# Attention scores with the matrix product in three fp16 parts, and half of the score sums on ScalarE

## The chip, the cores and the metric

The kernel runs on one core of a Trainium2 chip. The metric is the device time of one execution in microseconds (us), taken as the median of several runs. The core has a matrix engine (TensorE, in the profile PE), a vector engine (VectorE, DVE), an activation engine (ScalarE, ACT), a general engine that also issues the indirect DMAs (GpSimd, POOL) and an engine that issues plain DMAs and waits (SyncE, SP). The engines run their own instruction streams and meet at semaphores.

## The reference, cut to what matters

Four graph layers run over 3125 nodes with 64 features and 103125 edges sorted by destination. The change lies in the fourth layer, in its attention scores:

```python
h = jnp.maximum(_layernorm(x, axis=-1), 0.0)
gl = (h @ W_l).reshape(n, 6, 64)
gr = (h @ W_r).reshape(n, 6, 64)
s = jax.nn.leaky_relu(gl[src] + gr[dst], 0.2)
e = jnp.einsum('ehf,hf->eh', s, att)     # one score per edge and head
# softmax of e over the edges of each dst, then a weighted sum of gl[src]
```

## The kernel before, in words

The scores are made by `edge3a` (from line 1920). Edges are taken in tiles of 128 and batches of eight tiles (B = 8, 1024 edges); 101 batches are used. Two batches make a pair t, and n = 2t + h + 1 is the batch number. For each batch:

- POOL gathers the rows of the source nodes with eight indirect DMAs (`Gather.gather`, L892) into one of four buffers `src_rows`. Before a batch it waits in L890 for its indices, for `hcTp_ready` (the batch four before must have been turned, so that the buffer is free) and for the copy of that buffer to HBM.
- SP loads the destination numbers (L1957) and eight windows of node rows (L1960) for the batch after the next, once `hcTp_ready` says that the buffers are free. It also stores the gathered rows (`kept`, L1977) and loads gather indices (L878).
- PE `turn` (L2031, L2032): sixteen matmuls put the features of both ends of all edges of a batch, transposed, into PSUM (`both_ends_t_ps`, one buffer of 128 x 1024): destination rows picked out of the window by a one-hot matrix, source rows by the identity. Its last matmul increments `hcTp_ready`.
- ACT `turned` (L2079) copies that to SBUF (`both_ends_t`, fp32, two buffers) and increments `hcT_ready`.
- PE `project` (L2040): per tile one fp32 matmul of 128 x 128 by 128 x 396 (Wz: six heads of 66 columns), two tiles for each step q = 0 to 3, into two alternating PSUM buffers `z_ps`. It increments `z_ready`.
- DVE `weigh` (L2133): relu of z times `att_z`, one instruction of 128 x 792 for each q, into `terms`; increments `terms_ready`, which frees the `z_ps` buffer.
- DVE `sum_terms` (L2141): a reduce over the 66 columns for half a batch, twice in a batch, into `scores`; it increments `summed`.
- PE `turn_scores` (L2047) turns the scores of the batch before, ACT copies them out of PSUM (L2085) and issues their store (L2087).
- DVE also makes the one-hot matrix of the batch after the next (L2125) and copies eight window numbers (L2118).

The order on PE within the body of batch n is written out by hand: project 0, project 1, turn of batch n + 1, turn_scores of n - 1, project 2, project 3. PE increments its semaphores in that order. DVE's order is weigh 0, weigh 1, sum, one-hot, weigh 2, weigh 3, sum. ACT's is `turned` of n + 1, then the store of n - 1.

## Time and profile before

| | us |
|---|---|
| median of three runs | 6714.87 |
| lowest and highest run | 6709.61, 6737.81 |
| the profiled execution | 6677.32 |
| its span (first to last instruction) | 6675.1 |
| the score stage in it, from the first gather (4624.65) to the last DVE sum (5908.85) | 1284.2 |
| busy in the span: PE, DVE, POOL, ACT | 4704.2, 4170.2, 3155.2, 1888.7 |

A row of the timeline gives the start in us from the span's start, the duration, the engine, the source line, the operation, output and inputs, how many instructions are merged into it, and in brackets how long the engine was idle before it and what ended that. The releaser in brackets is inferred. A wait named "DMA edge_edge_attr<-in_ea" in this stage is put under the name of a transfer of another stage. An fp32 matmul stands in the trace as two records. Matmul starts are recorded, their ends are modelled. PEclk is the granted clock of TensorE in tenths of full speed: it has two levels, 1.2 and 2.4 GHz, and a number in between is the mean of a stretch.

### The profile page before, as it was taken

What the parts mean: (1) busy time and instruction counts of PE and PEld (TensorE: products, weight loads), DVE (VectorE), ACT (ScalarE), POOL (GpSimd) and SP (SyncE); (2) the same over time, 40 slices, a digit from 0 to 9 for tenths busy, and PEclk for the clock granted to TensorE, in tenths of its full rate; (3) what the DMA queues carried; (4) which work ended last, traced back from release to release, by engine and by line L of the source; (5) the groups of instructions that cost most, each with busy time, mean ns of one, the idle gap of its engine ahead of it and who ended that gap; (6) DMA issues with size and microseconds to landing.
All of it is one profiled execution on the core that took longest, in us unless ns stands there. A gap on an engine that the chain in (4) does not pass through costs nothing. (4 is left out here: it accounts for less than half of the span.)

```text
span 6675.1 us, 100965 instructions
## 1 busy us (share of the span) xinstructions
PE 4704.2 (70%) x28624; PEld 3007.3 (45%) x28624; DVE 4170.2 (62%) x7653; ACT 1888.7 (28%) x6318; POOL 3155.2 (47%) x2946
## 2 busy tenths in 40 slices
PE   3777777777777676667566666663777777739998
PEld 2333333333334333333344554452444444418997
DVE  4454444444446666666666666664666766688997
ACT  1333333333333000000133333331000000016775
POOL 3433343333331655555354454452666666515554
PEclk7778787888888788888677878886999888869999
DMA  3222222222221111111111111111443334411111
GB/s 84 55 54 51 53 56 52 52 51 54 55 54 32 38 38 38 39 39 36 26 41 38 41 40 38 41 40 32 108 111 108 110 110 117 110 49 51 49 49 34
DMA packets 492408, 379.08 MB, mean 57 GB/s; under 512 B 345930, under 2 KB 378971, under 8 KB 492339
## 3 DMA queue, kind: packets, MB, share of 16 engines
q1 hardware_dynamic: 394803, 288.65, 15.3%
q0 software_dynamic: 90560, 83.37, 7.0%
q10 hardware_dynamic: 6976, 6.23, 0.3%
q8 instruction: 33, 0.54, 0.0%
q14 instruction: 36, 0.29, 0.0%
HBM read 341.76 MB, written 36.12 MB: 57 GB/s over the span
## 5 line engine op out<-in xcount | busy, mean ns | idle before, releaser
L1009 POOL DMA_INDIRECT edge_src_rows<-table_wh,edge_gather_idx x806 | 787.1, 977 | 1169.5 <-DVE edge_small L1128 924.6
L1038 PE MATMUL edge_sums_ps<-edge_onehot_src,edge_halves 128*128 128x512 bf16 x4840 | 1048.3, 361 | 302.5 <-issue 296.5
L892 POOL DMA_INDIRECT edge3a_src_rows<-table_h,edge3a_gather_idx x808 | 764.3, 946 | 564.1 <-issue 311.2
L2040 PE MATMUL edge3a_z_ps<-Wz,edge3a_both_ends_t 128*128 128x396 f32 x1616 | 695.3, 579 | 365.2 <-DVE edge3a_terms L2133 315.1
L1114 DVE TENSOR_SCALAR edge_onehot_src<-layer_node_row,edge_src_col,edge_magnitude 128x1568 bf16<-128x1568 f16 x605 | 410.5, 679 | 842.8 <-remote 471.6
L892 POOL DMA_INDIRECT table_cat<-table_hn,table_gather_idx x592 | 599.5, 1013 | 631.6 <-PE edge_cat_t_ps L1720 340.4
L1401 POOL DMA_INDIRECT edge_src_rows<-table_h,edge_gather_idx x608 | 606.9, 998 | 553.9 <-PE edge_msg_ps L1433 190.8
L1038 PEld LDWEIGHTS edge_sums_ps<-edge_onehot_src,edge_halves 128*128 128x128 f16 x4840 | 428.0, 104 | 872.7 <-issue 537.7
L2133 DVE SCALAR_TENSOR_TENSOR edge3a_terms<-edge3a_z_ps,att_z 128x792 f32<-128x792 f32 x404 | 386.0, 977 | 406.1 <-DMA edge_edge_attr<-in_ea 223.9
L2040 PEld LDWEIGHTS edge3a_z_ps<-Wz,edge3a_both_ends_t 128*128 128x128 f32 x1616 | 333.5, 217 | 670.1 <-DVE edge3a_terms L2133 359.6
L2452 PE MATMUL edge3b_sums_ps<-edge3b_onehot,edge3b_weighted 128*128 128x128 f32 x4848 | 572.7, 278 | 6.2 <-DVE layers_accT L2490 4.5
L2452 PEld LDWEIGHTS edge3b_sums_ps<-edge3b_onehot,edge3b_weighted 128*128 128x128 f32 x4848 | 553.5, 193 | 11.8 <-DVE layers_accT L2490 4.7
L1416 PE MATMUL edge_src_rows_t_ps<-edge_onehot_src,edge_h_halves 128*128 128x512 f16 x1300 | 375.1, 431 | 230.4 <-DVE edge_onehot_src L1522 149.2
L2369 POOL TENSOR_TENSOR edge3b_weighted<-edge3b_src_rows,edge3b_alpha 128x1920 f32<-128x1920 f32 x101 | 350.3, 3468 | 344.9 <-DVE edge3b_alpha L2469 251.2
L2418 ACT ACTIVATE edge3b_weighted<-edge3b_src_rows,edge3b_alpha 128x64 f32<-128x64 f32 x1818 | 445.1, 334 | 166.1 <-DVE edge3b_alpha L2469 157.3
L1736 PE MATMUL edge_msg_ps<-rR,edge_cat_t 64*128 64x128 f32 x1616 | 180.7, 388 | 371.8 <-DVE edge_u L1861 255.4
L1066 ACT ACTIVATE edge_dst_rows<-edge_dst_rows_ps 128x390 f32<-128x390 f32 x153 | 70.4, 460 | 1293.1 <-DMA scores_by_head<-setup_zeros 928.5
L2079 ACT ACTIVATE edge3a_both_ends_t<-edge3a_both_ends_t_ps 128x1024 f32<-128x1024 f32 x101 | 103.5, 1024 | 1161.9 <-DMA edge_edge_attr<-in_ea 690.4
L1038 PE MATMUL edge_sums_ps<-edge_onehot_src_act,edge_halves 128*128 128x512 bf16 x1608 | 336.6, 340 | 77.0 <-issue 76.6
L2141 DVE TENSOR_REDUCE edge3a_scores<-edge3a_terms 128x24 f32<-128x1584 f32 x202 | 364.5, 1805 | 7.0
L1023 PE MATMUL edge_dst_rows_ps<-edge_window,edge_onehot_t 128*128 128x65 f32 x1632 | 263.0, 314 | 121.8 <-issue 82.8
L1875 DVE TENSOR_TENSOR layers_accT<-layers_accT,edge_sums_ps 65x128 f32 x808 | 198.7, 280 | 236.7 <-remote 217.7
(372 smaller groups left out, 8320.9 us busy)
## 6 DMA issues: line engine op xcount, KB each, us to landing
edge_dst_row<-in_dst_row SPq DMA_DIRECT2D x102, 512.0 KB
edge3a_dst_row<-in_dst_row SPq DMA_DIRECT2D x102, 512.0 KB
edge_window<-table_wh SPq DMA_DIRECT2D x816, 32.5 KB
edge3a_window<-table_h SPq DMA_DIRECT2D x816, 32.0 KB
edge_edge_attr<-in_ea SPq DMA_DIRECT2D x101, 256.0 KB
kept_rows<-edge3a_src_rows SPq DMA_DIRECT2D x101, 256.0 KB
edge3b_src_rows<-kept_rows SPq DMA_DIRECT2D x101, 256.0 KB
edge_edge_attr<-in_ea SPq DMA_DIRECT2D x101, 128.0 KB
```

What stands on the lines that cost most here:

```text
L892: nc.gpsimd.indirect_dma_start(self.slot(b, j), None, self.table[:, :], bass.IndirectOffsetOnAxis(ap=self.idx[b][:, j:j + 1], axis=0)).the ...
L1009: nc.gpsimd.indirect_dma_start(g[q][:, j, :], None, k.t_wh[:, :], bass.IndirectOffsetOnAxis(ap=idx[q][:, j:j + 1], axis=0)).then_inc(gathe ...
L1038: mm = pe.matmul(acc[:, i, 0:w], halves[q][:, j, a, :, :].rearrange("p h d -> p (h d)"), hot[:, o:o + w], start=first and a == 0, stop=False)
L1114: dve.tensor_scalar(slot_v(q, j)[:, :], k.node_row[:, :], col[q][:, j:j + 1], mag[q][:, j:j + 1], ALU.is_equal, ALU.mult).then_inc(hot_v, 1)
L1401: nc.gpsimd.indirect_dma_start(g[p][:, j, :], None, k.t_h[:, :], bass.IndirectOffsetOnAxis(ap=idx[p][:, j:j + 1], axis=0)).then_inc(gather ...
L1416: mm = pe.matmul(rowsTp[:, o:o + 512], h16[:, b, :], ring[b % RING][:, o:o + 512], start=(b == 0), stop=(b == NB - 1))
L2040: mm = pe.matmul(zp[q % 2][:, i, 0:H * ZH], hcT[h][:, j * P:(j + 1) * P], k.Wz[:, :], start=True, stop=True)
L2133: dve.scalar_tensor_tensor(terms[:, 2 * q:2 * q + 2, :], zp[q % 2][:, :, 0:H * ZH], 0.0, rows_over(k.att_z[:, :], 2), ALU.max, ALU.mult).t ...
L2141: dve.tensor_reduce(scs[h][:, :, j:j + B // 2].rearrange("p h b -> p b h"), terms[:, j:j + B // 2, :].rearrange("p b (h f) -> p b h f", h= ...
L2369: return engine.tensor_tensor(hp[h][:, a:b, :, :], rows, weights, ALU.mult)
L2418: w = act.activation(hp[h][:, j, a, :], st[h][:, j, :], ACT.Copy, scale=al[h][:, a, j:j + 1])
L2452: mm = pe.matmul(sums[j % 4][:, i, :], hp[h][:, j, 2 * i:2 * i + 2, :].rearrange("p a d -> p (a d)"), oh[h][:, j, :], start=True, stop=True)
```

## The change

The product with Wz is made from 16-bit parts. Both Wz and the turned rows are scaled by powers of two (LIFT is 4096; Wz also by a power of two found from its largest magnitude) and split into a high fp16 part and a low fp16 part, the rest. Three fp16 matmuls per tile, high by high, high by low and low by high, accumulate in PSUM in place of one fp32 matmul. ACT makes the high part of the rows (as before, but into fp16 and scaled). DVE makes the low part with a new instruction `lower` of 128 x 1024, which reads PSUM and the high part; PE's projections wait for it. The scales are taken back in `att_z`. A chain of small steps over ACT, DVE and PE before the first batch finds the power of two and splits Wz; PE's first `turn` stands behind it. The sums over the 66 columns are divided: DVE reduces tiles 0 to 3, and ACT sums tiles 4 to 7 with 24 ACTIVATEs of 128 x 66 that write their sum through `accum_out`. `turn_scores` and the later `weigh` wait for both.

```diff
-                        mm = pe.matmul(zp[q % 2][:, i, 0:H * ZH], hcT[h][:, j * P:(j + 1) * P],
-                                       k.Wz[:, :], start=True, stop=True)
+                        out, cols = zp[q % 2][:, i, 0:H * ZH], slice(j * P, (j + 1) * P)
+                        pe.matmul(out, hiT[h][:, cols], Whi[:, :], start=True, stop=False)
+                        pe.matmul(out, hiT[h][:, cols], Wlo[:, :], start=False, stop=False)
+                        mm = pe.matmul(out, loT[h][:, cols], Whi[:, :], start=False, stop=True)
...
                 def turn_scores(n, h):
                     pe.wait_ge(scT_ready, n)
-                    pe.wait_ge(summed, 2 * n + 4)
+                    pe.wait_ge(summed, n + 2)
+                    pe.wait_ge(summed_act, n + 2)
...
+                pe.wait_ge(most_ready, 1)
+                pe.matmul(scTp[0:1, 0:P], most[:, 0:1], k.ident[:, :], start=True, stop=True).then_inc(most_turned, 1)
+                pe.wait_ge(power_ready, 1)
+                pe.matmul(zp[0][:, 0, 0:1], ones[:, :], most[0:1, 2:3], start=True, stop=True).then_inc(power_spread, 1)
+                pe.wait_ge(W_ready, 2)
                 turn(1, 0, 1, 0, 0)
...
-                    act.activation(hcT[h][:, :], hcTp[:, :], ACT.Copy).then_inc(hcT_ready, 1)
+                    act.activation(hiT[h][:, :], hcTp[:, :], ACT.Copy, scale=LIFT).then_inc(hi_ready, 1)
+
+                def sum_terms(n, h):
+                    act.wait_ge(scTp_ready, n)
+                    for q in (2, 3):
+                        act.wait_ge(terms_ready, 4 * (n - 1) + q + 3)
+                        for j in (2 * q, 2 * q + 1):
+                            for f in range(H):
+                                last = act.activation(terms[:, j, f * ZH:(f + 1) * ZH], terms[:, j, f * ZH:(f + 1) * ZH], ACT.Copy,
+                                                      accum_out=scs[h][:, f, j:j + 1])
+                    last.then_inc(summed_act, 1)
...
+                        sum_terms(n, h)
...
-                    dve.wait_ge(summed, 2 * n + q // 2 + 1)
+                    dve.wait_ge(summed if q < 2 else summed_act, n + 1)
...
+                def lower(n, h):
+                    dve.wait_ge(hi_ready, n)
+                    dve.scalar_tensor_tensor(loT[h][:, :], hcTp[:, :], LIFT, hiT[h][:, :], ALU.mult,
+                                             ALU.subtract).then_inc(hcT_ready, 1)
...
                         weigh(n, 2)
+                        if not empty(last, h + 1):
+                            lower(n + 1, 1 - h)
                         weigh(n, 3)
-                        sum_terms(n, h, 1)
```

## Rows read from the trace of the kernel before

**Rows 1.** The page: busy time of each engine, and the clock in 40 slices.

```profile
PE 4704.2 (70%) x28624; PEld 3007.3 (45%) x28624; DVE 4170.2 (62%) x7653; ACT 1888.7 (28%) x6318; POOL 3155.2 (47%) x2946
PEclk7778787888888788888677878886999888869999
```

**Rows 2.** Groups by line, 4700 to 5900 us: busy, mean ns | idle before, releasers.

```profile
L892 POOL DMA_INDIRECT edge3a_src_rows<-table_h,edge3a_gather_idx x756 | 715.1, 946 | 454.6 <-issue 288.4 <-DMA edge_edge_attr<-in_ea 141.3 <-DMA kept_rows<-edge3a_src_rows 15.2
L2040 PE MATMUL edge3a_z_ps<-Wz,edge3a_both_ends_t 128*128 128x396 f32 x1563 | 672.5, 579 | 326.9 <-DVE edge3a_terms L2133 307.8 <-issue 18.8
L2133 DVE SCALAR_TENSOR_TENSOR edge3a_terms<-edge3a_z_ps,att_z 128x792 f32<-128x792 f32 x391 | 373.7, 977 | 359.6 <-DMA edge_edge_attr<-in_ea 217.9 <-PE edge3a_z_ps L2040 89.2 <-issue 52.1
L2141 DVE TENSOR_REDUCE edge3a_scores<-edge3a_terms 128x24 f32<-128x1584 f32 x196 | 353.7, 1805 | 6.7
L2125 DVE TENSOR_TENSOR edge3a_onehot_t<-edge3a_dst_row,edge3a_window_nodes_ps 128x1024 f32<-128x1024 int32 x98 | 118.6, 1211 | 0.0
```

**Rows 3.** Timeline of POOL: last and first gathers of two batches.

```profile
5306.15 0.95 POOL L892 DMA_INDIRECT edge3a_src_rows<-table_h,edge3a_gather_idx  x1 [0.30 <-issue]
5309.69 0.95 POOL L892 DMA_INDIRECT edge3a_src_rows<-table_h,edge3a_gather_idx  x1 [2.59 <-DMA edge_edge_attr<-in_ea]
5318.45 0.95 POOL L892 DMA_INDIRECT edge3a_src_rows<-table_h,edge3a_gather_idx  x1 [0.30 <-issue]
5321.65 0.95 POOL L892 DMA_INDIRECT edge3a_src_rows<-table_h,edge3a_gather_idx  x1 [2.26 <-issue]
```

**Rows 4.** Timeline of PE, same batch: last matmul of the turn, then projections 2 and 3.

```profile
5304.83 0.27 PE L2032 MATMUL edge3a_both_ends_t_ps<-ident,edge3a_src_rows 128*64 128x128 f32 x1
5305.25 3.23 PE L2040 MATMUL edge3a_z_ps<-Wz,edge3a_both_ends_t 128*128 128x396 f32 x8
```

**Rows 5.** Timeline of DVE and ACT, same batch.

```profile
5303.24 0.98 DVE L2133 SCALAR_TENSOR_TENSOR edge3a_terms<-edge3a_z_ps,att_z 128x792 f32<-128x792 f32 x1 [1.14 <-issue]
5308.98 1.02 ACT L2079 ACTIVATE edge3a_both_ends_t<-edge3a_both_ends_t_ps 128x1024 f32<-128x1024 f32 x1 [11.08 <-PE edge3a_z_ps L2040]
5309.08 1.87 DVE L2133 SCALAR_TENSOR_TENSOR edge3a_terms<-edge3a_z_ps,att_z 128x792 f32<-128x792 f32 x2 [1.90 <-PE edge3a_z_ps L2040]
5310.31 0.73 ACTq L2087 DMA_DIRECT2D scores_by_head<-edge3a_scores_t  x1
```

**Rows 6.** Timeline at the stage's start: PE, POOL, ACT.

```profile
4639.21 0.42 PE L2032 MATMUL edge3a_both_ends_t_ps<-ident,edge3a_src_rows 128*64 128x128 f32 x1
4663.42 0.95 POOL L892 DMA_INDIRECT edge3a_src_rows<-table_h,edge3a_gather_idx  x1 [0.30 <-issue]
4669.61 1.02 ACT L2079 ACTIVATE edge3a_both_ends_t<-edge3a_both_ends_t_ps 128x1024 f32<-128x1024 f32 x1 [54.05 <-DMA edge_edge_attr<-in_ea]
```

**Rows 7.** Timeline at the stage's end: POOL's last gather, then PE and ACT.

```profile
5868.33 0.94 POOL L892 DMA_INDIRECT edge3a_src_rows<-table_h,edge3a_gather_idx  x1 [0.30 <-issue]
5878.55 0.27 PE L2032 MATMUL edge3a_both_ends_t_ps<-ident,edge3a_src_rows 128*64 128x128 f32 x1
5878.95 1.02 ACT L2079 ACTIVATE edge3a_both_ends_t<-edge3a_both_ends_t_ps 128x1024 f32<-128x1024 f32 x1 [6.63 <-PE edge3a_both_ends_t_ps L2032]
5886.88 1.03 ACT L2079 ACTIVATE edge3a_both_ends_t<-edge3a_both_ends_t_ps 128x1024 f32<-128x1024 f32 x1 [6.75 <-PE edge3a_both_ends_t_ps L2032]
```

**Rows 8.** Timeline of ACT elsewhere: sums through `accum_out`, and small ACTIVATEs within SBUF.

```profile
3435.89 0.22 ACT L1756 ACTIVATE edge_squares<-edge_msg_ps 128x64 f32<-128x64 f32 x1
3435.99 0.20 ACT L1756 ACTIVATION_READ_ACCUMULATOR edge_squares<-edge_msg_ps 128x1 f32 x1
3436.08 0.23 ACT L1756 ACTIVATE edge_squares<-edge_msg_ps 128x64 f32<-128x64 f32 x1
6105.15 4.41 ACT L2418 ACTIVATE edge3b_weighted<-edge3b_src_rows,edge3b_alpha 128x64 f32<-128x64 f32 x18 [1.41 <-DVE edge3b_alpha L2469]
```

**Rows 9.** Nearest relatives of the new work: fp16 matmuls, and a DVE instruction on PSUM.

```profile
2200.44 0.60 PE L1416 MATMUL edge_src_rows_t_ps<-edge_onehot_src,edge_h_halves 128*128 128x512 f16 x2 [0.72 <-DVE edge_onehot_src L1522]
L1526 DVE TENSOR_TENSOR edge_onehot<-dst_rel,edge_columns_ps 128x1024 f32<-128x1024 f32 x101 | 123.3, 1221 | 350.8 <-remote 320.8 <-PE edge_sums_ps L1443 28.4
```

More of the change, by code:

```diff
@@ L1928, in edge3a @@
         oht = [c.sb(f"onehot_t{h}", [P, ROWS]) for h in (0, 1)]
-        hcT = [c.sb(f"both_ends_t{h}", [P, ROWS]) for h in (0, 1)]
+        hiT = [c.sb(f"both_ends_high{h}", [P, ROWS], F16) for h in (0, 1)]
+        loT = [c.sb(f"both_ends_low{h}", [P, ROWS], F16) for h in (0, 1)]
+        Wz = c.sb("Wz_scaled", [P, H * ZH])
+        Whi = c.sb("Wz_high", [P, H * ZH], F16)
+        Wlo = c.sb("Wz_low", [P, H * ZH], F16)
+        ones = c.sb("ones", [1, P])
+        most = c.sb("largest", [P, 4])
+        prep, abs_ready, most_ready, most_turned, power_ready, power_spread, scaled_ready, W_ready = c.sems(
+            "prep_step", "magnitudes_ready", "largest_ready", "largest_in_psum", "power_ready", "power_in_psum",
+            "scaled_ready", "Wz_parts_ready")
+        hi_ready, summed_act = c.sems("high_ready", "terms_summed_by_scalar")
         terms = c.sb("terms", [P, B, H * ZH])
@@ L2088, in store @@
                                   scT[h][:, :]).then_inc(stored[h], 16)
+                act.activation(Wz[:, :], k.Wz[:, :], ACT.Abs).then_inc(abs_ready, 1)
+                act.wait_ge(scaled_ready, 1)
+                act.activation(Whi[:, :], Wz[:, :], ACT.Copy).then_inc(W_ready, 1)
                 turned(1, 0)
@@ L2135, in weigh, with sum_terms @@
                                              ).then_inc(terms_ready, 1)
-                def sum_terms(n, h, half):
-                    dve.wait_ge(terms_ready, 4 * (n - 1) + 2 * half + 4)
+                def sum_terms(n, h):
+                    dve.wait_ge(terms_ready, 4 * (n - 1) + 4)
                     dve.wait_ge(scTp_ready, n)
-                    j = half * B // 2
-                    dve.tensor_reduce(scs[h][:, :, j:j + B // 2].rearrange("p h b -> p b h"),
-                                      terms[:, j:j + B // 2, :].rearrange("p b (h f) -> p b h f", h=H),
+                    dve.tensor_reduce(scs[h][:, :, 0:B // 2].rearrange("p h b -> p b h"),
+                                      terms[:, 0:B // 2, :].rearrange("p b (h f) -> p b h f", h=H),
@@ L2143, in sum_terms @@
                                       AX, ALU.add).then_inc(summed, 1)
+                def lower(n, h):
+                    dve.wait_ge(hi_ready, n)
+                    dve.scalar_tensor_tensor(loT[h][:, :], hcTp[:, :], LIFT, hiT[h][:, :], ALU.mult,
+                                             ALU.subtract).then_inc(hcT_ready, 1)
+                step = Chain(dve, prep)
+                step(dve.memset(ones[:, :], 1.0))
+                dve.wait_ge(abs_ready, 1)
+                dve.tensor_reduce(most[:, 0:1], Wz[:, :], AX, ALU.max).then_inc(most_ready, 1)
@@ new lines, in _ @@
+                dve.wait_ge(most_turned, 1)
+                step(dve.tensor_reduce(most[0:1, 1:2], scTp[0:1, 0:P], AX, ALU.max))
+                dve.tensor_scalar(most[0:1, 2:3].bitcast(I32), most[0:1, 1:2].bitcast(I32), EXPONENT, LEAST,
+                                  ALU.bitwise_and, ALU.bitwise_or).then_inc(power_ready, 1)
+                dve.wait_ge(power_spread, 1)
+                step(dve.tensor_copy(most[:, 0:1], zp[0][:, 0, 0:1]))
+                step(dve.tensor_scalar(most[:, 3:4].bitcast(I32), most[:, 0:1].bitcast(I32), EXPONENT, None,
+                                       ALU.bitwise_xor))
@@ L2145, in _ @@
+                dve.tensor_scalar(Wz[:, :], k.Wz[:, :], most[:, 3:4], LIFT, ALU.mult, ALU.mult).then_inc(scaled_ready, 1)
+                step(dve.tensor_scalar(k.att_z[:, :], k.att_z[:, :], most[:, 0:1], 0.5 / (LIFT * LIFT),
+                                       ALU.mult, ALU.mult))
+                dve.wait_ge(scaled_ready, 1)
+                dve.wait_ge(W_ready, 1)
+                dve.tensor_tensor(Wlo[:, :], Wz[:, :], Whi[:, :], ALU.subtract).then_inc(W_ready, 1)
                 nodes(1, 0, 0)
@@ L2148, in _ @@
                 onehot_t(2, 1, 0)
+                lower(1, 0)
                 def body(t, last):
```

7 lines of the change are left out of this document (4 added, 3 removed).

## The prediction

> **What bounds the kernel now.** The page comes first [rows 1]: no engine is busy throughout, and TensorE's clock is granted at eight tenths of full speed or more in most slices, so nothing can be read off the shares. The change lies in one stage, so the groups by line of its steady part come next [rows 2]. In 1200 us DVE makes 98 one-hots, one for each batch: a batch takes 12.2 us. The same rows give each engine's work per batch. POOL: 8 gathers. DVE: 4 x 0.977 + 2 x 1.805 + 1.21 and 0.16 for a small copy = 8.9 us. PE: the eight records of four fp32 projections start 0.33 us apart, 0.66 us for each tile [rows 4], so 5.3 us of projections, plus a turn. ACT: little. None of DVE, PE or ACT fills 12.2 us.
>
> The timeline of POOL tells what does [rows 3]. Seven steps lead from the first gather of a batch at 5309.69 to its last at 5318.45: 1.25 us each, 9.7 us from the first start to the last end at 5319.40. Then POOL waits 2.26 us and starts again at 5321.65. The batch before is alike: last end 5307.10, next start 5309.69, 2.59 us. So a period of 12.0 us is 9.7 of gathers and 2.3 of waiting, and POOL waits for the turn of an earlier batch.
>
> Why is that turn late? By PE's own rows it isn't: its last matmul starts at 5304.83 and lasts 0.27, yet ACT, which waits for just this, wakes at 5308.98 [rows 4, 5]. DVE's weigh 2, which needs a projection recorded well before, wakes 0.1 us behind ACT, and weigh 3 follows with no gap [rows 5]. So the increments that PE owes from the turn onward (turn, scores, projections 2 and 3) all arrive in one burst, 1.9 us after POOL's last gather of the batch ended. The projections ahead of the turn arrive without such a delay: weigh 1 starts at 5303.24, amid gathers [rows 5]. The stage's two ends show that the gathers hold the burst back. At the start the first turn's last matmul is over at 4639.63, every engine but POOL is idle, and ACT wakes at 4669.61, after the last of 32 gathers, which ended at 4664.37 [rows 6]: 30 us of hold. At the end, with the last gather over at 5869.27, the turn's last matmul ends at 5878.82 and ACT starts at 5878.95: no hold, and the batches then come 7.93 us apart [rows 7]. I can't name the mechanism; the pattern is that a turn's increment becomes visible only when the outstanding gathers are done. That makes a lockstep: release, 0.7 us, eight gathers, 1.5 to 1.9 us, release. No engine's speed enters it as long as the turn is ready when the gathers finish.
>
> **The change part by part**, from a release R (5308.98 is one) to the next at R + 12.0.
>
> ACT makes the high part: 1.02 us, as now. Its score copy and DMA issue are over at 5311.04, R + 2.1 [rows 5]. DVE does weigh 2 to R + 1.1, then `lower`. The trace has none; its nearest row is a DVE instruction of 128 x 1024 that reads PSUM, 1.22 us [rows 9]. It ends at R + 2.4, where PE could start before at R + 1.1: 1.3 us later. Against that one reduce of 1.8 us goes, so DVE has 8.9 - 1.8 + 1.2 = 8.3 us of work. Bounds of `lower`: 0.98 us, one weigh of 792 columns, and 1.8 us, one reduce.
>
> PE: 24 fp16 matmuls for a batch in place of 8 fp32 ones. Two fp16 matmuls of 512 columns take 0.60 us, the last of them to its modelled end of 0.38, so 0.22 us apart [rows 9]; by columns 396/512 x 0.22 = 0.17 us. A tile costs 0.51 instead of 0.66, a batch 4.1 instead of 5.3. Upper bound: weight loads that don't overlap and a pitch of 0.32 as between the fp32 records, 7.7 us. The chain is then: project 0 from R + 2.4 to 3.4, project 1 (after weigh 3, R + 3.4) to 4.5, the turn, 1.7 us, to R + 6.2. It has to be done by R + 12.0: 5.8 us of slack. If the lighter load keeps the clock at its low level of 1.2 GHz, projections take 2.0 each and the turn 3.4: R + 9.9, still inside.
>
> ACT's 24 sums: in the two-instruction form that `accum_out` makes, starts of pairs are 0.19 to 0.20 us apart (3435.89 to 3436.08) though each lasts 0.22 and 0.20: they overlap [rows 8]. So 24 x 0.20 = 4.8 us, from R + 2.1 to R + 7.0 (the terms come at R + 1.1 and 3.4). Those rows read PSUM; the new ones read and write SBUF. The nearest row for that, 18 ACTIVATEs in 4.41 us, gives (4.41 - 0.33)/17 = 0.24 us apart [rows 8]; with the read's step of 0.1 on top 0.34, and 24 x 0.34 = 8.2, to R + 10.3. I take 0.20 to 0.34: both end before R + 12.0. Behind these sums are queued, on ACT, the next batch's high part, and on PE turn_scores and with it projections 2 and 3. At 0.20 scores follow at R + 7.1 and projection 3 is over by R + 9.5. At 0.34 it is over at about R + 12.6, where DVE wants it at R + 14.5 (after weigh 2 and `lower`). Nobody waits. The cover of all this is the hold; without it the chain would be DVE's 8.3 us or POOL's 10.0.
>
> The Trainium skill ("VectorE: DVE Perf Modes", section on the TRN2 errata of SBUF-source ops) speaks against moving many small sums to ScalarE: it gives 224 cycles fixed for SBUF to SBUF and 172 for PSUM to SBUF. By an estimate from that page a pair would be 52/1.2 = 43 ns dearer than the PSUM rows, 24 of them 1.0 us, and ACT would end at R + 8.0 and not 7.0; the sum would stay.
>
> Steady part: 98 batches x 0 us. Head: the steps that split Wz, a dozen small ones, some 6 us from 4621, lie ahead of a turn that starts near 4636 and is released at 4669.6 [rows 6]: 0. Should PE's two increments of this chain be held by the gathers as the turn's are, the first turn would come after 4669.6: + 8. That has a reason against it, projections aren't held. Tail: once POOL has stopped, three batches run at 7.93 us [rows 7], bound by DVE. There DVE saves 0.6 us a batch, `lower` stands between the release and the projections (up to 1.2 each), and the last 12 sums take 2.4 where the reduce took 1.8: between -2 and + 3, taken as 0. Sum: 0 us, with bounds of -2 and + 11.
>
> The profiled execution took 6677.3 us, 37.6 under the median of the runs; its new span would be 6675. On the median that is 6714.9, and I say 6715. About 0.5% (34 us) is what a measurement of this kernel can tell from no change; the runs themselves lie 28 us apart.
>
> **Rivals.** *ACT becomes the bound (slower).* From a pair of (12.0 - 2.1)/24 = 0.41 us upward ACT fills the period. If the accumulator read waits for its ACTIVATE and the next waits for it, a pair costs 0.24 + 0.23 = 0.47 us from the single durations: 2.1 + 11.3 = 13.4 us a batch, + 1.4 x 98 = 137 us, 6850. Against it: the overlapping starts [rows 8]. For it: reading and writing the same SBUF tile has no row.
>
> *The hold is not the gathers' but the pace of the chain (faster).* If PE's recorded starts mislead and its real work fills the time up to the burst, 1.2 us less of projections per batch shorten it: 6715 - 1.2 x 98 = 6597. If the hold vanished, POOL's 10.0 us would be the floor, 2.0 x 98 = 196 us less, 6519. Against it: 30 us of hold at the start with PE idle, and none at the end [rows 6, 7].
>
> *The projections don't get cheaper (no change).* At 0.32 us per fp16 matmul PE works 7.7 us instead of 5.3 and the turn is over near R + 8: the same 6715. Only the profile would show it.
>
> **How the numbers follow.** Forecast, with the third rival in it: 0.77. ACT-bound or a similar new wait: 0.12. Chain-bound or hold gone: 0.11. Range 6678 to 6752: the forecast's own, from the sum at the profiled execution's level (6677) to the highest run (6738) with the + 11 of the bounds; it leaves the two other cases out, which are too far to reach. Faster by over 0.5% 0.11, within 0.77, slower 0.12.
>
> **What would show it.** Right: gathers still 8 x 1.25 us with a gap of 2.3 to 2.6; ACT's high part still starts 1.5 to 1.9 us after the last gather; PE's turn recorded 4 us or more before; 24 pairs 0.20 to 0.34 us apart; PE's busy time in the stage down by a fifth; DVE's by 0.6 us a batch. Wrong: gathers waiting over 3 us while ACT is busy up to the next high part, or a gap of 0.3 us between batches on POOL, which would mean that the hold depended on the work that was changed.

## The result, and the profile after

The changed kernel takes 6836.97 us (median of 4 runs, 6821.48 to 6846.83) beside 6712.24 of before: a ratio of 1.0173, 95% interval 1.0147 to 1.0200, 125 us slower. Forecast were 6715 us and a range to 6752. The profiled executions took 6821.48 and 6677.32 us, 144 apart. From its first gather (4622.4) to its last instruction (6053.3) the score stage takes 1430.9 us; before it took 1285.0 by the same marks. No other stage changed by more than 23 us, in either direction.

The page, busy times and clock, to be held against [rows 1]:

```profile
PE 4677.8 (69%) x29284; PEld 2963.8 (43%) x29436; DVE 4109.1 (60%) x7662; ACT 2542.5 (37%) x11168; POOL 3147.6 (46%) x2946
PEclk6888888888787878887688788777877777868999
```

The groups by line, 4700 to 5900 us, to be held against [rows 2]:

```profile
L892 POOL DMA_INDIRECT edge3a_src_rows<-table_h,edge3a_gather_idx x694 | 656.4, 946 | 544.6 <-issue 270.5 <-DMA kept_rows<-edge3a_src_rows 211.3 <-PE edge3a_both_ends_t_ps L2042 62.9
L2105 ACT ACTIVATE edge3a_terms<-edge3a_terms 128x66 f32<-128x66 f32 x2077 | 505.6, 245 | 372.9 <-issue 320.7 <-DVE edge3a_terms L2166 50.1
L2166 DVE SCALAR_TENSOR_TENSOR edge3a_terms<-edge3a_z_ps,att_z 128x792 f32<-128x792 f32 x346 | 338.2, 979 | 508.3 <-remote 358.2 <-issue 124.8 <-PE edge3a_z_ps L2053 24.9
L2051 PE MATMUL edge3a_z_ps<-edge3a_Wz_high,edge3a_both_ends_high 128*128 128x396 f16 x690 | 294.5, 427 | 54.4 <-issue 43.1 <-DVE edge3a_both_ends_low L2179 11.4
L2158 DVE TENSOR_TENSOR edge3a_onehot_t<-edge3a_dst_row,edge3a_window_nodes_ps 128x1024 f32<-128x1024 int32 x87 | 105.3, 1210 | 0.0
```

87 one-hots in 1200 us instead of 98: 13.8 us a batch. PE and DVE are busy for a smaller share of the time, ACT for a larger one. POOL's gathers still last 946 ns, but its idle time rose from 454.6 to 544.6 us for fewer gathers, and a releaser that counted 15.2 us before now counts 211.3: the store of the gathered rows. ACT has a new idle time of 320.7 us, "issue", ahead of its sums and between them.

What that is shows in the timeline of ACT, sums of one batch (start, duration, [idle before]):

```profile
5305.03 0.24 ACT L2105 ACTIVATE edge3a_terms<-edge3a_terms 128x66 f32<-128x66 f32 x1
5305.27 0.24 ACT L2105 ACTIVATE edge3a_terms<-edge3a_terms 128x66 f32<-128x66 f32 x1
...
5307.58 0.26 ACT L2105 ACTIVATE edge3a_terms<-edge3a_terms 128x66 f32<-128x66 f32 x1 [0.50 <-issue]
5307.75 0.19 ACT L2105 ACTIVATION_READ_ACCUMULATOR edge3a_terms<-edge3a_terms 128x1 f32 x1
5308.32 0.26 ACT L2105 ACTIVATE edge3a_terms<-edge3a_terms 128x66 f32<-128x66 f32 x1 [0.39 <-issue]
5309.04 0.20 ACT L2105 ACTIVATION_READ_ACCUMULATOR edge3a_terms<-edge3a_terms 128x1 f32 x1 [0.46 <-issue]
5309.77 0.26 ACT L2105 ACTIVATE edge3a_terms<-edge3a_terms 128x66 f32<-128x66 f32 x1 [0.52 <-issue]
...
5313.14 1.00 ACT L2097 ACTIVATE edge3a_both_ends_high<-edge3a_both_ends_t_ps 128x1024 f16<-128x1024 f32 x1
...
5317.15 0.26 ACT L2105 ACTIVATE edge3a_terms<-edge3a_terms 128x66 f32<-128x66 f32 x1 [2.76 <-issue]
```

Pairs start 0.24 us apart, and then, from 5305.3 on, single instructions come 0.7 us apart (8.32, 9.04, 9.77), though each lasts a quarter of that and waits for no semaphore. I call these late steps. They end 1.5 us after POOL's last gather:

```profile
5299.10 0.94 POOL L892 DMA_INDIRECT edge3a_src_rows<-table_h,edge3a_gather_idx  x1 [5.20 <-DMA kept_rows<-edge3a_src_rows]
...
5309.43 0.95 POOL L892 DMA_INDIRECT edge3a_src_rows<-table_h,edge3a_gather_idx  x1 [0.30 <-issue]
5313.03 0.94 POOL L892 DMA_INDIRECT edge3a_src_rows<-table_h,edge3a_gather_idx  x1 [2.66 <-issue]
```

So what the prediction had seen as PE's increments held back is one face of something that slows ACT too, and SP: in the trace of before, from 4740 to 5560 us, 248 of the steps between SP's own instructions are 0.64 to 0.78 us long, and on a chip without late steps (e11 below, a stretch of 800 us) 15. In the batch above the turn's last matmul was recorded at 5307.25 and its count came at 5312.24. That is how it went throughout before (the count 4.85 us after the last record, median of 66 batches, the turn's records 1.70 us from first to last), but in the changed kernel it is the exception, 8% of the batches. In most, as in the next one, PE itself can be seen to stall inside the turn, whose records then stretch over 4.0 us (median of 59) with the count right behind them (timeline of PE):

```profile
5321.87 0.38 PE L2041 MATMUL edge3a_both_ends_t_ps<-edge3a_onehot_t,edge3a_window 128*64 128x128 f32 x2
5323.70 0.27 PE L2042 MATMUL edge3a_both_ends_t_ps<-ident,edge3a_src_rows 128*64 128x128 f32 x1 [1.45 <-issue]
5324.42 0.31 PE L2042 MATMUL edge3a_both_ends_t_ps<-ident,edge3a_src_rows 128*64 128x128 f32 x1 [0.45 <-issue]
```

**Where the 1.5 us of a batch lie.** Its eight gathers take 9.7 us in every kernel (once in some twelve batches a gap of 1.9 us falls behind the first of them, the same in all kernels), so a batch grows by POOL's pause between the batches alone. I cut each pause between 4740 and 5560 us in two, at the time when the turn's count (`hcTp_ready`) rises: from the end of the last gather to the count, and from the count to POOL's next start. Means in us, 60 to 66 pauses each, worked out from the semaphores' times in the traces; kernels named e are the experiments below; "late in sums" is by how much the steps from the first sum's start to the last one's exceed 0.24 us a pair. (With 24 sums the step from the twelfth to the thirteenth is in it, where ACT can also wait for weigh 3; without that step the changed kernel has 3.1.)

| kernel | pause | to the count | count to POOL | late in sums |
|---|---|---|---|---|
| before | 2.51 | 1.63 | 0.88 | |
| e1, three fp16 products, sums on DVE | 2.95 | 1.85 | 1.10 | |
| e2, fp32 products, sums on ACT | 3.44 | 2.11 | 1.33 | 3.3 |
| changed | 3.99 | 2.42 | 1.57 | 4.2 |
| e3, changed, scores turned last | 3.82 | 2.04 | 1.79 | 4.9 |
| e5, before without window loads | 2.68 | 1.86 | 0.82 | |
| e6, changed without window loads | 3.17 | 2.35 | 0.82 | 3.4 |
| e15, changed, 12 sums on ACT | 3.54 | 1.99 | 1.56 | 0.3 |
| e17, changed, kept rows stored earlier | 3.74 | 2.56 | 1.19 | 4.0 |

Of the 1.48 us by which the pause grew, 0.79 lie ahead of the count and 0.69 behind it.

### The profile page after: what moved, and what is told of

It reads as the page before. It is cut to its first block and busy times, and to the rows that moved or that the text cites. A ratio compares the mean times of both kernels' runs of the same rounds, so it can differ in the third digit from the quotient of the medians.

```text
span 6819.3 us, 107297 instructions
## 1 busy us (share of the span) xinstructions
PE 4677.8 (69%) x29284; PEld 2963.8 (43%) x29436; DVE 4109.1 (60%) x7662; ACT 2542.5 (37%) x11168; POOL 3147.6 (46%) x2946
## 5 line engine op out<-in xcount | busy, mean ns | idle before, releaser
L1038 PE MATMUL edge_sums_ps<-edge_onehot_src,edge_halves 128*128 128x512 bf16 (+1 forms) x4736 | 983.1, 354 | 213.8 <-issue 201.3
L2105 ACT ACTIVATE edge3a_terms<-edge3a_terms 128x66 f32<-128x66 f32 x2424 | 589.7, 245 | 421.1 <-issue 344.8
L2105 ACT ACTIVATION_READ_ACCUMULATOR edge3a_terms<-edge3a_terms 128x1 f32 x2424 | 457.6, 189 | 171.6 <-issue 171.0
L1416 PE MATMUL edge_src_rows_t_ps<-edge_onehot_src,edge_h_halves 128*128 128x512 f16 x1300 | 360.0, 418 | 183.3 <-DVE edge_onehot_src L1522 119.3
L1038 PE MATMUL edge_sums_ps<-edge_onehot_src_act,edge_halves 128*128 128x512 bf16 (+1 forms) x1560 | 338.6, 336 | 206.0 <-issue 201.3
L2051 PE MATMUL edge3a_z_ps<-edge3a_Wz_high,edge3a_both_ends_high 128*128 128x396 f16 x808 | 342.6, 424 | 101.6 <-DVE edge3a_both_ends_low L2179 52.0
L1486 ACT ACTIVATE edge_msg<-edge_msg_ps 128x512 f32<-128x512 f32 x101 | 60.3, 597 | 864.9 <-remote 597.6
L1077 ACT ACTIVATE edge_onehot_src_act<-edge_distance,edge_magnitude,edge_minus_magnitude 128x1568 bf16<-128x1568 f16 x201 | 340.4, 1694 | 15.6 <-PE edge_sums_ps L1038 5.3
```

Of the source, the lines that this page charges most:

```text
L1038: mm = pe.matmul(acc[:, i, 0:w], halves[q][:, j, a, :, :].rearrange("p h d -> p (h d)"), hot[:, o:o + w], start=first and a == 0, stop=False)
L1416: mm = pe.matmul(rowsTp[:, o:o + 512], h16[:, b, :], ring[b % RING][:, o:o + 512], start=(b == 0), stop=(b == NB - 1))
L2051: pe.matmul(out, hiT[h][:, cols], Whi[:, :], start=True, stop=False)
L2105: last = act.activation(terms[:, j, f * ZH:(f + 1) * ZH], terms[:, j, f * ZH:(f + 1) * ZH], ACT.Copy, accum_out=scs[h][:, f, j:j + 1])
```

## The experiments

They ran on several chips; each time is held against the kernel before on its own chip. Stages and batches, though, are read from one profiled execution of each kernel, and for the kernel before there is one such trace, from another chip.

### Which half of the change costs: e1, e2

e1 is the changed kernel with

```
-                        sum_terms(n, h)
...
+                        sum_terms(n, h, 1)
```

(the first line is ACT's, the second stands behind weigh 3 on DVE, for tiles 4 to 7) and e2 the kernel before with only the opposite edit.

> The changed kernel, but VectorE makes both halves of the sums again; the three fp16 products, the high and low parts and their scales stay. Theory A (the change's time comes from ScalarE's 24 sums, which lie in the chain sums, turning of the scores, projection 2, weigh 2, sums): about 6712 us as before, batches of edge3a 12.1 to 12.3 us. Theory B (the three-part product, its extra low-part step on VectorE and the lower granted clock are what costs): about 6835 us. If both carry something it lies between, near 6712 plus B's share.

> The kernel before (fp32 products), with one edit alone: ScalarE sums the terms of tiles 4 to 7. Theory A: the whole loss comes, 6835 us or somewhat more, with the same gaps between ScalarE's sums. Theory B: 6712 us or less, since VectorE is relieved of 1.8 us a batch and nothing else changes.

Measured beside 6659.65: e1 6729.12, ratio 1.0089 (1.0059 to 1.0119); e2 6763.25, ratio 1.0154 (1.0123 to 1.0186). The stage takes 1336.0 and 1381.3 us. Against 1285.0 of before that is 51 and 96 us; together 147, where the whole change costs 146. By the medians it is 69 and 104 us, together 173, where the whole change costs 125 (128 in e13). So both halves cost, and neither theory stands alone: some three fifths come with the sums, two fifths with the products. That the two add up exactly isn't shown.

### Is it the chain over the scores: e3

```
-                        if not (first and h == 0):
-                            turn_scores(n - 1, 1 - h)
                         project(n, h, 2)
                         project(n, h, 3)
+                        if not (first and h == 0):
+                            turn_scores(n - 1, 1 - h)
```

> The changed kernel, with PE's turning of the last batch's scores put behind projection 3 instead of ahead of projection 2, so that projections 2 and 3 no longer wait for ScalarE's 24 sums of the batch before. Theory A1 (it is that chain): the chain is broken at PE; weigh 2 still waits for the buffer that ScalarE read, but ahead of that the projection is done; 12.3 to 13.0 us a batch, 6715 to 6780 us. Theory A2 (ScalarE as such is full: its own work and its gaps make 13.7 us a batch in whatever order): 6835 us, unchanged.

6792.54 us, ratio 1.0204 (1.0171 to 1.0237), stage 1406.8, batch 13.6: A1's range is missed, and A2's "unchanged" came, though e15 will show that ACT isn't full. In the changed kernel PE waited for ACT's sums ahead of that step (5.85 us before turn_scores at 5313.38). With the wait moved, the table shows the count as early as in e15, and POOL even later behind it. The wait passed from PE to DVE: weigh 2 needs the tiles that ACT still sums, and by the waits of e3 (4700 to 5500 us) the weigh steps wait 178.6 us for ACT, in 52 batches, a wait that isn't among those of the changed kernel.

### Gathers: e4, and the same kernel without a pause between gathers, e12 and e14

e4: the changed kernel, `Gather` issues 4 gathers a batch instead of 8, all waits on them count 4. e12 and e14 are one kernel: before, but the gathers fill tiles that nobody reads, and POOL waits only for its own gathers of four batches ago:

```
-        wait_past(pool, self.free, 2 * t + h - 1)
-        if kept:
-            wait_past(pool, kept[b], 16 * m)
+        wait_past(pool, ga.gathered[b], B * 16 * m)
...
-                self.slot(b, j), None, self.table[:, :],
+                gd[b][:, j, :], None, k.t_h3[:, :],
```

> The changed kernel with 4 gathers a batch in edge3a instead of 8 (the rows of tiles 4 to 7 stay zero). Theory H (the stretch in which PE's count isn't let go and in which ScalarE's sums come 0.4 to 0.7 us apart ends 1.7 to 1.9 us behind the last gather, whatever makes it): that stretch ends 5 us sooner, the sums come 0.24 us apart almost throughout, and the batch falls by at least the 3 to 5 us that the gaps take, to 9 to 10.5 us: 6835 - 98 x 3.5 = about 6490 us. Rival (gaps and gathers only fall together by chance): the gaps stay, the batch stays near 13.7 us and the time near 6835 us.

e4: 6371.25 us beside 6659.65, 288 us less than before though it has all the sums. A batch takes 9.4 us; from the turn's first record to its count 2.0 us pass (median), where it is 6.8 before and 4.7 in the changed kernel; the sums lose 0.8 us a batch. Groups by line, 4700 to 5500 us:

```profile
L2111 ACT ACTIVATE edge3a_terms<-edge3a_terms 128x66 f32<-128x66 f32 x2045 | 494.4, 243 | 164.2 <-issue 136.4 <-DVE edge3a_terms L2172 27.5
L893 POOL DMA_INDIRECT edge3a_src_rows<-table_h,edge3a_gather_idx x341 | 322.5, 946 | 477.6 <-DMA kept_rows<-edge3a_src_rows 383.4 <-issue 85.1 <-PE edge3a_both_ends_t_ps L2048 9.0
```

> The kernel before, but edge3a's gathers fill tiles that nobody reads, and POOL waits for nothing but its own earlier gathers, so that it gathers without a pause from the stage's start (the turn reads constant tiles, the scores are of wrong rows). Theory K taken literally (PE's counts are held as long as any gather is under way): PE's counts come out only in the rare pauses, and the stage takes longer than its 1282 us, if it doesn't take twice as long. Rival M (a count is held only until the gathers that were queued at the time are done, or the hold needs the handshake between PE and POOL): the batches run at VectorE's pace of 8.5 to 9 us while POOL gathers at 10 us a batch, and the stage takes some 1010 us by POOL: about 6390 us.

> The kernel with unpaced gathers again (tiles that nobody reads, POOL waits for its own earlier gathers alone, the turn reads constant tiles), for a chip on which the kernel before takes some 6700 us. Theory K (PE's counts are late as long as any gather is under way): the stage takes longer than 1282 us. Rival M (the lateness needs the handshake between PE and POOL): the stage takes some 1010 us. On a chip without late counts it says nothing new: 1009 us as before.

e12 met a chip without late steps (below) and says nothing on them: 8.4 us a batch, VectorE's pace. e14 met one that has them: 7345.97 us beside 6736.61. The view by windows, first while POOL gathers without a pause, then after its last gather (busy us of PE, PEld, DVE, ACT, POOL; granted clock, DMA share, GB/s):

```profile
4650.00:5650.00 1000.00, 126.25 (x380) 58.50 (x380) 60.10 (x57) 9.80 (x14) 753.17 (x731) 0.52 0.16 34
5900.00:6500.00 600.00, 561.98 (x3554) 341.39 (x3552) 595.13 (x571) 83.58 (x142) 0.00 (x0) 1.00 0.42 130
```

and PE's timeline in the first:

```profile
5012.50 0.82 PE L2058 MATMUL edge3a_z_ps<-Wz,edge3a_both_ends_t 128*128 128x396 f32 x1 [2.01 <-issue]
5015.30 0.82 PE L2058 MATMUL edge3a_z_ps<-Wz,edge3a_both_ends_t 128*128 128x396 f32 x1 [1.98 <-issue]
5018.10 0.82 PE L2058 MATMUL edge3a_z_ps<-Wz,edge3a_both_ends_t 128*128 128x396 f32 x1 [1.98 <-issue]
```

Matmuls come 2.80 us apart, four steps of 0.7 (an fp32 projection has two loads and two matmuls), a batch takes 140 us, and once the gathers are over 8.4 us. PE waits for no semaphore between these matmuls, POOL doesn't look at its count, and the source rows that it turns are constant tiles. So gathers in a long row are enough to make PE's late steps; e4 shows that four in a row, with a pause behind them, make hardly any.

### Do the other transfers make them: e5 to e8

e5 and e6 are before and changed with the window tiles loaded for the first two batches only; e7 and e8 load 8 columns of dst_row instead of 1024 from the third batch on:

```
-                    for j, base in enumerate(window_starts(nc, k, SP, t, h)):
+                    for j, base in enumerate(window_starts(nc, k, SP, t, h)) if begin else ():
```

> The kernel before, but edge3a loads the 8 window tiles only for its first two batches and turns those again and again (so SP issues 3 transfers a batch instead of 11 and reads no window starts; the scores are of wrong rows). Theory W (the spells in which SP's and ScalarE's own steps come 0.7 us apart, and PE's count is late, come from the window loads beside the gathers): the spells go, PE's count goes out with the turn, and the batch falls from 12.1 us to what the gathers alone take, 8 x 1.25 plus at most 1 us: some 10.5 us, 6660 - 98 x 1.6 = about 6500 us. Theory G (the gathers alone make them): 12.1 us a batch and about 6660 us, unchanged.

> The same edit to the changed kernel. Theory W: ScalarE's 24 sums come 0.24 us apart throughout; batch 10.5 to 12 us, 6500 to 6650 us. Theory G: 13.7 us a batch, about 6810 us.

> The kernel before, but from the third batch on the load of dst_row brings 8 columns instead of 1024 (32 KB read and written instead of 512 KB; the one-hots of edge3a stay those of the first batches). Theory D (the spells come from the bytes that move beside the gathers): the spells shrink or go, 10.5 to 11.5 us a batch, 6500 to 6600 us. Theories W and G: unchanged, 12.1 us and about 6660 us.

> The same edit to the changed kernel. Theory D: batch below 12.5 us, below 6700 us. Theories W and G: 13.7 us a batch, about 6810 us.

Beside 6757.7: e5 6704.28, e6 6764.63, e7 6722.23, e8 6862.96, one run each, that of before too. Theories W and D fall: from the turn's first record to its count 3.9 us or more pass in all four (median), the batch of e5 is 12.5 us and not 10.5, and ACT's sums still lose 3.4 us in e6, beside 4.3 in e8. But e6 is faster than e8 by 98 us and has 13.0 us a batch, and the table says where: the count is as late as in the changed kernel, yet POOL starts 0.82 us behind it and not 1.57. Without window loads the change costs 60 us (e6 less e5), and all of it lies ahead of the count; with them it costs 141 (e8 less e7). POOL's waits, 4700 to 5500 us, show what is missing (us in total, times, longest): changed kernel, then e6:

```profile
POOL edge3a_src_rows L892 <- DMA kept_rows<-edge3a_src_rows: 135.4, 28, 5.6
POOL edge3a_src_rows L892 <- PE edge3a_both_ends_t_ps L2042: 45.6, 14, 3.5
```

```profile
POOL edge3a_src_rows L892 <- PE edge3a_both_ends_t_ps L2042: 96.6, 30, 3.9
```

The same view gives 4.6 us for that store before the change, 87.8 in e1 and 112.3 in e2. SP's queue explains it: the store stands behind eight window loads, which SP issues only when the count has come, and if these fall into late steps, the store goes out late. The timeline of SP in the changed kernel shows one such round:

```profile
5312.40 0.33 SPq L1967 DMA_DIRECT2D edge3a_dst_row<-in_dst_row  x1
5313.56 5.09 SPq L1970 DMA_DIRECT2D edge3a_window<-table_h  x8
5321.54 0.72 SPq L878 DMA_DIRECT2D edge3a_gather_idx<-in_src_t  x1
5324.38 0.00 SPq L1987 DMA_DIRECT2D kept_rows<-edge3a_src_rows  x1
```

and POOL, whose last gather had ended at 5322.73, starts again at 5325.79, released by that store.

### Sums and store, one at a time: e15, e17

e15 leaves 12 of the 24 sums on ACT, e17 issues the store one batch earlier in SP's queue:

```
-                    for q in (2, 3):
+                    for q in (3,):
...
-                                     g[b][:, :, :]).then_inc(kept[b], 16)
+                            keep(*behind_one(t, q, m, h))
```

> The changed kernel with half as much on ScalarE: it sums tiles 6 and 7 (12 pairs), VectorE sums tiles 0 to 5 (the second piece, tiles 4 and 5, behind weigh 3). Theory A' (the batch goes round by ScalarE: hi part 1.0, wait for low part and weigh 2 some 3, then the 24 sums, 5.8 by themselves and 2.7 of late steps): 12 pairs fewer take 2.9 us and half of the late steps out of the ring, 13.8 - 4.2 = 9.6, so that the gathers' handshake bounds again with what the fp16 products add: 12.4 to 12.7 us a batch as with all sums on VectorE, ratio 1.007 to 1.012. Theory B' (the loss of the sums' half is made by the extra hand-over between engines and not by the number of sums): 13.4 us a batch or more, ratio 1.015 or more.

> The changed kernel, with the store of the gathered rows (kept_rows) issued one batch earlier in SP's queue. In the changed kernel POOL waits 135 us of the 800 us from 4700 on for that store, 2 us a batch, against 5 us in all in the kernel before; it stands in SP's queue behind 8 window loads whose steps come 0.7 us apart while gathers run. Theory N (most of the loss comes by that store: everything behind PE is a little later, SP's loads fall into the late steps, the store lands late and POOL starts the next gathers late): a batch takes about 12.6 to 12.9 us instead of 13.8, ratio 1.005 to 1.010. Theory A' (ScalarE's ring of 24 sums bounds, POOL's wait is only another face of it): unchanged, 13.7 us, ratio 1.017 to 1.019.

e15: 6760.64 beside 6659.93, ratio 1.0155 (1.0129 to 1.0181). The changed kernel has 1.0173, and 1.0189 in e13; these intervals overlap, so the times alone don't show a gain. The batch takes 13.4 us. The sums now lie ahead of the late steps and lose 0.3 us a batch, ACT's high part starts 0.1 us behind the count and no longer 1.7 us, and the count is 0.43 us earlier, but POOL's start behind it is as late as in the changed kernel. That is the forecast of B' (13.4 us or more, ratio 1.015 or more): ACT's ring of sums doesn't carry the loss by itself. The view of POOL's waits puts 144.8 us of 800 to the store again; by which way the handed-over sums make it late here wasn't traced. e17: 6834.76 beside 6717.78, ratio 1.0148 (1.0096 to 1.0200), an interval that takes in the changed kernel. POOL's wait for the store is gone and another entry of SP's queue has taken its place (same view, 4700 to 5500 us):

```profile
POOL edge3a_src_rows L892 <- DMA edge3a_gather_idx<-in_src_t: 105.7, 24, 5.1
POOL edge3a_src_rows L892 <- PE edge3a_both_ends_t_ps L2049: 91.1, 27, 3.9
```

Behind the count POOL starts 0.38 us earlier than in the changed kernel, but the count is 0.14 us later. So each experiment takes a part away and neither brings the batch down to what its theory forecast: A' wanted 12.4 to 12.7 us in e15 (measured 13.4), N wanted 12.6 to 12.9 us in e17 (measured 13.6).

### A chip without late steps: e9, e10, e11

e9 is the changed kernel with the turn behind projection 3 and `lower` behind weigh 3; e10 and e11 are before with

```
-                        mm = pe.matmul(hcTp[0:D, cols], g[b][:, j, :], k.ident[:, :], start=True, stop=True)
+                        mm = pe.matmul(hcTp[0:D, cols], win[h][:, j, :], k.ident[:, :], start=True, stop=True)
```

and

```
-                    pe.wait_ge(ga.gathered[b], B * 16 * (m + 1))
+                    pe.wait_ge(seen, n)
```

where `seen` is a count of SP's, which waits for the gathers.

> The changed kernel with the turn of the next batch moved behind projection 3 on PE, and the step that makes the low part moved behind weigh 3 on VectorE (it needs that turn). Theory K (PE's count of whatever stands at or behind the turn goes out 1.6 to 2.5 us after the last gather; what stands ahead of the turn isn't held): weigh 2, weigh 3 and ScalarE's sums then run while POOL gathers, nothing but the turn waits for the gathers' end, and a batch takes 12.1 to 12.6 us: 6660 to 6720 us beside 6660 of before. Rival L (whatever PE does while gathers are under way is late, turn or not): projections 2 and 3 are held as well and the batch stays at 13.5 us or more, 6800 us.

> The kernel before, but the turn's 8 source products read the window tile of the same batch instead of the gathered rows (same shapes, same waits; the scores are of wrong rows). Theory R (PE is held because it reads the tiles that gathers fill): the count of the turn comes with its last record instead of 4.8 us behind it, POOL starts 3 to 5 us sooner, batch 10.4 us at most, about 6500 us. Theory K (only that gathers are under way): count still 1.6 us after the last gather, 12.1 us a batch, about 6660 us.

> The kernel before, but PE doesn't wait for the gathers' own count: SyncE waits for it and adds 1 to a count of its own, on which PE waits. Theory S (PE's wait on a count that transfers raise is what holds it): the count of the turn comes with its last record, batch 10.4 us, about 6500 us. Theory K: still 1.6 us after the last gather, 12.1 us a batch or somewhat more, since SyncE passes the count on late, 6660 to 6720 us.

On this chip the kernel before takes 5228.47 us (5225.61 to 5230.73), 22% less than on the others. e11 took 5230.73 and e10 5224.85. The groups of e11, 3500 to 4300 us:

```profile
L892 POOL DMA_INDIRECT edge3a_src_rows<-table_h,edge3a_gather_idx x642 | 605.8, 944 | 195.7 <-issue 194.1 <-PE edge3a_both_ends_t_ps L2034 1.5
```

642 gathers in 800 us: one every 1.25 us with no pause between batches, 9.98 us a batch. The turn's count in e11 comes 0.01 us after its last record (median), and the sums of e9 lose 0.0 us. The first stage, which has no part in the change, takes 1312 us here and 2031 in the trace of before, from its first gather to its last matmul. So the late steps belong to the chips, not to the kernel alone, and e10 and e11 couldn't tell what triggers them. e9 itself took 5708.17, ratio 1.0917 (1.0899 to 1.0936): with the turn last, nothing overlaps the way turn, high part, low part, projection. Its waits, 3500 to 4300 us:

```profile
ACT edge3a_both_ends_high L2097 <- PE edge3a_both_ends_t_ps L2042: 360.6, 54, 7.5
PE edge3a_z_ps L2051 <- DVE edge3a_both_ends_low L2179: 137.4, 54, 2.6
```

K and L gave no such case. The changed kernel itself wasn't run on such a chip; what it is worth there is open. An estimate from the traces is that it would lose nothing in the steady part: 3.8 us from the end of one batch's sums to the start of the next one's (changed kernel) and 5.9 us for 24 sums without late steps (e9) make 9.7 us, just under the 9.98 that the gathers take there.

### The changed kernel again, and two attempts to gain: e13, e16, e18

> The changed kernel itself, unchanged, beside the kernel before on this chip, since the last chip ran the kernel before in 5228 us, 22% below the 6715 us of the prediction, with POOL's gathers 1.25 us apart without a pause and no late counts. Theory P (the change's loss is a matter of late counts and 0.7 us steps): on a chip that shows none, the changed kernel is no slower than before (the batch goes by POOL at 10.0 us), ratio 0.99 to 1.01; on a chip that shows them, ratio 1.015 to 1.025. Rival C (the chain turn of the scores, projection 2, weigh 2, sums is longer than a batch by itself): slower on either, and on a chip without late counts by more, since a batch there has only 10.0 us: stage of 1300 us or more beside 1024, ratio above 1.04.

6864.93 beside 6736.61, ratio 1.0189 (1.0163 to 1.0215), 13.9 us a batch: the result repeats in another set of runs, on a chip with late steps. That is the half of theory P that could be tested; its other half, and C, need a chip without them.

e16 puts a wait between the fourth and fifth gather of before:

```
+            if kept and j == B // 2:
+                pool.wait_ge(self.gathered[b], B * 16 * m + 8 * B)
```

e18 adds the earlier store of e17.

> The kernel before with one wait in POOL's queue: between the fourth and the fifth gather of a batch it waits until the first four have landed. Theory Q (the late steps need more than some 4 gathers in a row, as half the gathers showed none): PE's counts aren't late any more and POOL never waits for them, so a batch takes 8 x 1.25 plus twice a landing of some 2 us: 12 to 14 us, and the count of the turn comes with its last record. Theory K (any gather under way makes PE late): the counts are late, and the pause comes on top: 14 us or more a batch, 6700 + 98 x 2 = 6900 us.

> The kernel before with the pause between POOL's fourth and fifth gather and the store of the gathered rows one batch earlier: with the pause alone POOL gathered 8 in a row across the batches' border and one look took 6645 us beside 6660. Theory N: what batches of 13 us and more there were (some 12 in 100, 1.5 us above the others) go to 12.0 us, 6630 to 6650 us beside 6660, ratio 0.995 to 0.998. Rival: no gain that can be told from before, 0.999 to 1.001, since those batches are long for another reason.

e16: 6645.43 in one run beside 6659.93, inside the spread of before's own runs (6641.98 to 6675.03). The pause took the place of the old one: POOL then gathers eight in a row across the border of two batches, and PE's count comes 4.3 us after the turn's last record (median). Q isn't borne out, but it wasn't tested either, since there never were four in a row. e18: 6715.83 beside 6717.78, ratio 0.9996 (0.9984 to 1.0007): no gain, where N forecast 0.995 to 0.998. Nothing here beats the kernel before on a chip with late steps.

## Why the prediction was wrong

**The bound of before was read rightly.** Gathers, pause, release: e4 and e14 confirm that it is the gathers that hold PE's counts. The head was right as well: from the first gather to the first high part 45.1 us, before 45.0. The tail wasn't: from the end of the last gather to the end of the stage 50.4 us pass and before 40.4, 10 more where + 3 was the bound. The other 136 of the stage's 146 us lie between the first gather and the last, mostly in the steady batches, for which the sum had 0. (The range, too, doesn't follow from its own terms: 6738 and the + 11 make 6749, not 6752. That changes nothing here.)

**The step that failed** is "both end before R + 12.0 ... Nobody waits". In the changed kernel the sums end 15.6 us after the release ahead of them (mean of 59 batches), that is 1.8 us after the next one, and ACT's high part, which was to start at the release, starts 1.7 us behind it. The prediction's own sign of being wrong came: gathers wait over 3 us (3.99) while ACT is busy up to the next high part. Three terms went wrong, none of them by the price of an operation:

- The start of the sums. "The terms come at R + 1.1" supposed projection 2 to be ready and merely held at R. Release 5312.4 (SP's next load is issued at 5312.40) finds ACT still summing until 5313.1 and turn_scores behind these sums, so projection 2 is issued only then and weigh 2 follows 3.7 us after R:

```profile
5313.38 0.63 PE L2060 MATMUL edge3a_scores_t_ps<-ident,edge3a_scores 128*48 128x128 f32 x2 [5.85 <-ACT edge3a_terms L2105]
5313.94 0.51 PE L2051 MATMUL edge3a_z_ps<-edge3a_Wz_high,edge3a_both_ends_high 128*128 128x396 f16 x1
```

```profile
5316.14 0.98 DVE L2166 SCALAR_TENSOR_TENSOR edge3a_terms<-edge3a_z_ps,att_z 128x792 f32<-128x792 f32 x1 [5.88 <-issue]
```

  The sums start at R + 4.8 here, and 5.5 us after the count on average, and not at R + 2.1 [rows 4, 5]. The forecast followed one batch and took for granted that the batch before it had ended in time.
- Their length. A pair is 0.24 us, within 0.20 to 0.34, and 24 are 5.8 us. The late steps and the wait for weigh 3 add 4.2 on average, 10.1 us from the first start to the last end. 5.5 + 10.1 is the 15.6 above, beyond 12.0. The hold had been read as PE's alone; in the trace of before ACT had nothing to do in those stretches, so it couldn't show, and "the cover of all this is the hold" priced the work under it as if it ran undisturbed.
- What waits for the end. SP wasn't in the sum. In 1 of 66 pauses before, and in 29 of 60 after, POOL starts over 1.5 us behind the count. A release that comes later sends SP's eight loads and the store into the late steps, and the gathers wait for the store; what lies behind the count is nearly half of the loss (0.69 of 1.48 us). The rest lies ahead of it: the turn starts 7.4 us after the batch's first gather instead of 4.5 (means), so that more of it is left when the gathers end.

**`lower` as cover-priced.** It was forecast at 1.22 us and takes 1.215. It was costed at nothing behind 5.8 us of slack; with the products alone (e1) the batch is 0.5 us longer all the same, half of it ahead of the count and half behind. The turn then starts 5.8 us after the release before it instead of 5.1 (means), but only 0.2 us later after the batch's first gather, 4.7 instead of 4.5. The slack was counted to the end of the gathers as if nothing ahead of it slowed down; why so small a shift costs 0.5 us isn't shown.

**The product.** 0.17 us a matmul at the full clock, as forecast; but the mean granted clock from 4700 to 5900 us fell from 0.90 to 0.80, and 0.33 us apart, at the low level of 1.2 GHz, is nearly as frequent (5313.94 and on; 46% of the steps, against 52% at 0.17). PE's busy time in that window fell from 873 to 791 us, a tenth and not a fifth. The view by windows of before and of the changed kernel (columns as above):

```profile
4700.00:5900.00 1200.00, 873.15 (x4895) 512.03 (x4892) 834.07 (x782) 115.61 (x196) 714.95 (x756) 0.90 0.41 110
```

```profile
4700.00:5900.00 1200.00, 790.87 (x5023) 420.83 (x5019) 686.02 (x693) 664.93 (x4328) 655.70 (x694) 0.80 0.36 98
```

**The rivals.** "ACT becomes the bound" gave 6850 us and + 1.4 us a batch, and these are nearly the numbers that came (6837, + 1.5); its mechanism came only in part. It asked for 0.47 us a pair where the pair is 0.24, and for 0.41 to tip. With the late steps a pair comes to 10.1/24 = 0.42, right at that border, and with a start at 5.5 instead of 2.1 the border itself is lower: late steps and later start tipped it together. So ACT does end too late in the changed kernel, but e15 has it end in time and keeps most of the loss; the rival's number was met by luck in part. It stood at 0.12 and should have had more, since the forecast rested on two processes, sums and hold, which the trace of before never showed at once.

**The price of a pair.** The rows showed pairs on PSUM operands 0.19 to 0.20 us apart [rows 8] (median 0.197), the new ones on SBUF are 0.24 (median 0.240): 43 ns more. The Trainium skill ("VectorE: DVE Perf Modes", the TRN2 errata of SBUF-source ops) gives 52 cycles more for ScalarE's SBUF operands than for PSUM ones, by an estimate from that page 43 ns: the trace agrees.

What stays open: what the late steps are. Shown is that they come with long rows of gathers, in every set of runs but one, and on PE, ACT and SP. Whether the turn's reading of gathered tiles or PE's wait on the gathers adds to it wasn't measured on such a chip. What makes e1's 51 us isn't shown either, nor what keeps POOL late in e15; no experiment gave the whole loss back.

## What to carry to other kernels

A stall that covers work in the profile covers it only for the engines that were seen working in it; ask of idle engines whether their steps would be slow there too. Where a new piece of work closes a ring from one batch to the next, follow it through two batches, and set its end against the time when its own successor in the batch after needs it. And put every queue that starts transfers behind the moved release into the sum: here nearly half of the loss lay behind the release, where gathers waited for a store that stood behind eight loads.

## What the runs showed of the hardware

While POOL's indirect gathers follow each other every 1.25 us, instructions of PE, ACT and SP come 0.7 us apart: SP's in the kernel before mostly from the fourth gather of a row on, ACT's sums in the changed kernel first at the fifth to seventh (53 of 59 batches), until 1.5 to 2.5 us after the last gather. With gathers for 1000 us without a pause a batch took 140 us instead of 8.4. One chip showed none of it and ran the same kernel in 5228 instead of 6660 to 6760 us. And a matmul's record isn't proof that its result was there: before the change PE's rows of the turn look whole while its count comes 4.85 us later (median).
